# Attention and routed experts in one kernel: bias moved between scatter and return, a memset behind each return DMA, an unpaced scatter, and 13 attention batches ahead of the experts

## What is computed

```python
xn = layernorm(x)
q, k, v = split(xn @ w_qkv)                       # 16 heads of width 8
q_, k_ = exp(z - max(z)) with z = q @ proj, k @ proj   # 32 features per head
attn = (q_ @ (k_.T @ v)) / (q_ @ sum(k_) + 1e-6)
gates = sinkhorn((xn @ router_w.T + router_b) / temp, 3)
w, e = top_k(gates, 2)                            # weights normalised to sum 1
expert(t) = (relu(xn @ wg[e]) * (xn @ wp[e])) @ wo[e]
out = x + (attn @ w_out + b_out) + (xn + sum over the two experts of w * expert)
```

## Time and profile before

| | us |
|---|---|
| median of 3 runs | 329.74 (328.19 to 330.65) |
| the profiled execution | 327.3 |
| its span, first to last instruction | 325.5 |
| PE, DVE, ACT, POOL busy | 274.7, 222.9, 160.3, 237.6 |

### The profile page before, as it was taken

One profiled execution on the slowest core, in us unless ns is written; L12 is line 12 of the kernel. 1 busy time (PEld: TensorE's weight loads), 2 busy tenths in 40 slices (PEclk: granted clock), 3 DMA queues, 4 the chain that ended last, 5 costly groups with the idle time before them and its releaser, 6 DMA issues.

```text
span 325.5 us, 6627 instructions
## 1 busy us (share of the span) xinstructions
PE 274.7 (84%) x2044; PEld 257.5 (79%) x2044; DVE 222.9 (68%) x523; ACT 160.3 (49%) x365; POOL 237.6 (73%) x388
## 2 busy tenths in 40 slices
PE   5996878799999999999699999999999999850020
PEld 4896777689999999999599999999999999850010
DVE  4948889668888778888855777777777774500173
ACT  2774562134555555455346677777777775210000
POOL 5899520757888888888611688888888888888381
PEclk9998996589999999999979999999999999885555
DMA  7974000551111111111142598898888841111694
GB/s 236 339 272 164 4 0 0 167 191 45 47 50 52 45 49 46 47 50 51 36 110 61 166 244 245 244 256 251 245 246 248 251 134 48 42 49 40 226 383 174
DMA packets 32462, 45.22 MB, mean 139 GB/s; under 512 B 5328, under 2 KB 21200, under 8 KB 32432
## 3 DMA queue, kind: packets, MB, share of 16 engines
q1 hardware_dynamic: 26592, 33.83, 34.1%
q0 software_dynamic: 4544, 9.84, 9.0%
q10 hardware_dynamic: 1296, 1.20, 1.1%
HBM read 27.17 MB, written 17.68 MB: 138 GB/s over the span
## 4 chain that ended last, share of the span: by engine, by line
PE 49%; POOL 23%; DVE 12%; DMA 6%; issue 5%; ACT 2%; SPq 1%; ACTq 0%; POOLq 0%; DVEq 0%
POOL rows_y L541 17%; PE bank L642 7%; PE bank L666 6%; POOL acc L496 5%; PE bank L618 4%; PE bank L619 4%; PE bank L620 4%; PE bank L656 4%; PE bank L795 3%; DMA xn<-rows_y 2%; PE bank L591 2%; PE bank L783 2%; PE bank L574 2%; PE bank L784 2%; PE bank L785 2%
## 5 line engine op out<-in xcount | busy, mean ns | idle before, releaser
L541 POOL DMA_INDIRECT rows_y<-xn,row_i x78 | 80.5, 1032 | 28.2 <-ACT xn L969 15.1
L532 POOL DMA_INDIRECT slots_x<-xn,slot_i x64 | 63.9, 999 | 29.4 <-DVE slot_i L1195 10.1
L871 ACT ACTIVATE feat<-z_sb 128x512 f32<-128x512 f32 x64 | 39.9, 631 | 65.7 <-DVE z_sb L1065 65.7
L1058 DVE TENSOR_REDUCE neg_max<-bank 128x16 f32<-128x512 f32 x64 | 42.7, 684 | 19.8 <-PE bank L620 19.8
L783 PE MATMUL bank<-xT_high,w_high 128*128 128x256 f32 x156 | 47.3, 303 | 0.5 <-issue 0.5
L785 PE MATMUL bank<-xT_high,w_low 128*128 128x256 f32 x156 | 44.0, 282 | 0.0
L784 PE MATMUL bank<-xT_low,w_high 128*128 128x256 f32 x156 | 44.0, 282 | 0.0
L1065 DVE TENSOR_TENSOR z_sb<-bank,neg_max 128x512 f32<-128x512 f32 x64 | 42.6, 684 | 0.5
L795 PE MATMUL bank<-w_tile,hidden 128*128 128x128 f32 x312 | 41.0, 275 | 0.0
L642 PEld LDWEIGHTS bank<-v_aug,feat 128*128 128x128 f32 x256 | 31.5, 200 | 8.8 <-issue 7.4
L795 PEld LDWEIGHTS bank<-w_tile,hidden 128*128 128x128 f32 x312 | 38.2, 192 | 0.1
(11 more groups left out here) (145 smaller groups left out, 562.5 us busy)
## 6 DMA issues: line engine op xcount, KB each, us to landing
w_tile<-w_expert_dram SPq DMA_DIRECT2D x39, 384.0 KB
slots_x<-w_tile SPq DMA_DIRECT2D x39, 144.0 KB, 2.2
x_tile<-slots_x SPq DMA_DIRECT2D x39, 130.0 KB
acc<-x_dram SPq DMA_DIRECT2D x8, 256.0 KB, 5.3
xn<-rows_y SPq DMA_DIRECT2D x8, 256.0 KB, 5.8
w_tile<-rows_y SPq DMA_DIRECT2D x8, 256.0 KB, 6.5
rows_y<-xn,row_i POOLq DMA_INDIRECT x78, 3.7
slots_x<-xn,slot_i POOLq DMA_INDIRECT x64, 2.3
```

The costliest lines, as they stand in the source:

```text
L532: pool.indirect_dma_start(slots_x, bass.IndirectOffsetOnAxis(slot_i[k][:, i:i + 1], 0), xn[:, j, :], None).then_inc(scattered[n % FLIGHT], 16)
L541: pool.indirect_dma_start(rows_y, bass.IndirectOffsetOnAxis(row_i[:, k, t:t + 1], 0), y_tile(k, t), None)\
L871: act.activation(feat[par][n][:, :], z_sb[n][:, :], ACT.Exp).then_inc(feat_ready, 1)
L1058: dve.tensor_reduce(neg_max[n][:, :], args(n), AX_X, ALU.max, negate=True).then_inc(z_negmax, 1)
```

## The change

EARLY is 13 rather than 14. The scatter has no wait on `z_shifted` any more. `add_bias` adds the bias to a group of four tiles at once (eight calls of 128x512 in place of 64 of 128x64), all between the scatter and the first return, each call waiting for the attention additions that lie in its tiles and before (`acc_added`, at most 12). Behind each of the 78 return DMAs stands a memset and nothing else. `add_projection` waits for all eight bias groups at batch 12 only, and DVE's wait for the bias ahead of its combination is gone.

```diff
--- before.py
+++ after.py
@@ -58,13 +58,10 @@
     GROUP = 4
     NG = NT // GROUP
     BY_ACT = 2
-    LOOP_FROM = 2
     LINKS = 8
-    EARLY = 14
+    EARLY = 13
     FLIGHT = 4
     SETTLED = 24
-    PER_TWO = 10
-    LEAD = 1
     YR = 16
     UP = 3
     DX = D + 16
@@ -94,7 +91,7 @@
         scan_keep = sb("scan_keep", [P, E, NT])
         spare_row = sb("spare_row", [P, 2 * SLOT_TILES])
         eps_tile = sb("eps_tile", [P, 1])
-        gap = sb("gap", [P, SLOT_TILES])
+        gap = sb("gap", [P, 2 * SLOT_TILES])
 
         acc = sb("acc", [P, NT, D])
         xn = sb("xn", [P, NT, DX])
@@ -490,10 +487,10 @@
                 j, cols = half_tile(n)
                 pool.tensor_tensor(acc[:, j, cols], acc[:, j, cols], xn[:, j, cols], ALU.add).then_inc(base_added, 1)
 
-            def add_bias(n):
-
-                j, cols = half_tile((n + 4 * (EARLY - 1)) % (2 * NT))
-                pool.tensor_tensor(acc[:, j, cols], acc[:, j, cols], b_out_sb[:, cols], ALU.add).then_inc(bias_added, 1)
+            def add_bias(g):
+
+                tiles = acc[:, g * GROUP:(g + 1) * GROUP, :]
+                pool.tensor_tensor(tiles, tiles, over_tiles(b_out_sb, GROUP), ALU.add).then_inc(bias_added, 1)
 
 
             pool.wait_ge(weights_landed, 16 * N_WEIGHTS)
@@ -528,7 +525,6 @@
                         second_choice(SETTLED, NT, 1)
                     if n >= FLIGHT:
                         pool.wait_ge(scattered[n % FLIGHT], 16 * (n // FLIGHT))
-                    pool.wait_ge(z_shifted, 4 * LOOP_FROM - LEAD + 8 * n // PER_TWO)
                     pool.indirect_dma_start(slots_x, bass.IndirectOffsetOnAxis(slot_i[k][:, i:i + 1], 0),
                                             xn[:, j, :], None).then_inc(scattered[n % FLIGHT], 16)
                     add_xn(n)
@@ -540,17 +536,17 @@
                 for t in range(2):
                     pool.indirect_dma_start(rows_y, bass.IndirectOffsetOnAxis(row_i[:, k, t:t + 1], 0), y_tile(k, t), None)\
                         .then_inc(y_sent[k % YR], 16)
-                    n = 2 * k + t
-                    for piece in range(n * NT // SLOT_TILES, (n + 1) * NT // SLOT_TILES):
-                        add_bias(piece)
-                pool.memset(gap[:, k:k + 1], 0.0)
+                    pool.memset(gap[:, 2 * k + t:2 * k + t + 1], 0.0)
 
             pool.wait_ge(base_added, 2 * NT)
+            for g in range(NG):
+                pool.wait_ge(acc_added, min(GROUP // 2 * (g + 1), EARLY - 1))
+                add_bias(g)
             pool.wait_ge(acc_added, EARLY - 1)
             for k in range(SLOT_TILES):
                 send_rows(k)
 
-            pool.wait_ge(bias_added, 2 * NT)
+            pool.wait_ge(bias_added, NG)
             pool.wait_ge(acc_added, GROUP // 2 * (NG // 2))
             for n in range(NG // 2):
                 for k in range(TOPK):
@@ -1095,8 +1091,8 @@
             def add_projection(b):
                 dve.wait_ge(proj_ready, b + 1)
                 dve.wait_ge(base_added, 4 * b + 4)
-                if late(b, EARLY - 1):
-                    dve.wait_ge(bias_added, 2 * NT - 4 * (EARLY - 1))
+                if b == EARLY - 1:
+                    dve.wait_ge(bias_added, NG)
                 tiles = acc[:, bass.ds(2 * b, 2), :]
                 dve.tensor_tensor(tiles, bank[QT_BANK][:, 0:2 * P].rearrange("p (t d) -> p t d", t=2), tiles, ALU.add)\
                     .then_inc(acc_added, 1)
@@ -1314,7 +1310,6 @@
 
             for b in range(EARLY, NB):
                 step(b, b // 2, b % 2, front=b + 1 < NB)
-            dve.wait_ge(bias_added, 2 * NT)
             combine_group(0)
             denominators(NB - 1)
             invert(NB - 1)
```

## The result

The changed kernel took 339.3 us (median; 337.7 to 343.5) where the kernel before took 329.0 (327.9 to 330.7): 1.027 times its time, 95% interval 1.019 to 1.036. It is slower, though the interval leaves open whether by 2%. Foretold was 306. The rows of a run are from one recorded execution, and in `wide_memset`, `add_behind` and `add_1` further down that one was among the slower of its kernel (331.5, 327.6 and 350.9).

What follows compares the result with a forecast made beforehand. POOL's returns were taken to bound the kernel, and attention after the change: DVE free at 288.1 + 7.0 + 2.0 = 297.1, plus 5.1 to the span's end (302.2), 1.8 and 2.4, giving 306; range 302.5 to 310.

Steps and rivals of the forecast that it cites:

- New: every distance is 1.29, a pair 2.58, against PE's 2.545 a tile: Returns beside the experts: return DMAs 1.29 us apart, so POOL walks almost beside PE instead of falling behind 0.6 a tile.
- EARLY 13 and the scatter: Before the experts: they start 7.85 us earlier; without its wait the last scatter starts at 154.6, 9 us earlier.
- Bias in one place: Between scatter and first return: eight bias calls take 10.3 us, replacing 23.9, hidden in idle time with 2 to 3 left.
- The return: POOL's returns: third at 174.9, 75 distances of 1.29 are 96.8, plus 2.5 for holds; last starts at 274.1.
- The end: DVE's combination: attention, not the return, is late; DVE ends at 297.1, the span 5.1 later at 302.2.
- The own range: Whole kernel: the main forecast's median lies between 302.5 and 310 us, given 72%.
- Held every tile: Rival, returns beside the experts: DVE holds POOL's DMAs 0.6 in all 37 pairs, 22 us, median 323; at half, 312; 10%.
- The scatter's pace is its own: Rival, scatter: something other than the wait sets its pace, last scatter stays at 163.5, end some 8 later, median 314; 7%.
- Row loads late: Rival, experts' row loads: added latency makes PE wait; half a us more gives 314 (8%), 1.5 us more gives 331 (3%).
- 0.93 for faster: Whole kernel: the chance given that the change is faster by over 1%; within 1% had 0.03, slower 0.04.

Runs made afterwards that it cites:

- wide_memset: The changed kernel with a 128x256 memset behind each return DMA instead of the one-column memset, on chip A; its recorded execution took 331.5 us.
- add_behind: The changed kernel with a 128x64 addition, both inputs in SBUF, behind each return DMA instead of the memset, first on chip A; recorded execution 327.6 us.
- add_1: The changed kernel with a one-column addition behind each return DMA instead of the memset, on chip D; its recorded execution took 350.9 us.
- after_again: The changed kernel, unmodified, run again on chip C: 302.6 us.
- memset_320_2: The changed kernel with a 128x320 memset behind each return DMA, second run, on chip B (batch B2): 320.5 us.
- add_128: The changed kernel with a 128x128 addition behind each return DMA instead of the memset, on chip B (batch B2); time not given in the text.
- unpaced_before: The kernel before with only the scatter's wait on attention taken out, on chip C: 0.997 times the kernel before.
- no_memset: The changed kernel without the memsets behind the return DMAs, on chip A; time not given, 30 tiles held.
- copy_behind: The changed kernel with a one-column SBUF copy behind each return DMA instead of the memset, on chip B (batch B1); time not given in the text.
- half_rows: The changed kernel returning only half of each row, the other half left out of the output, on chip B (batch B1); time not given, 32 tiles held.
- add_behind_3: The changed kernel with the 128x64 addition behind each return DMA instead of the memset, run on chip B (batch B2): 322.7 us.

## Why the prediction was wrong

**The step that failed** is "New: every distance is 1.29, a pair 2.58, against PE's 2.545 a tile". The first half is right, the returns are 1.26 to 1.27 apart wherever they have work. The second carries PE's tile over from a trace in which no more than one distance in six was 1.29, each followed by longer ones, to a kernel in which all are. PE's tile was 3.37 us on average. Over the experts that is the 32.4 us above, 38 distances of 0.85 more than on C, and no term of the sum and no rival stood for it. What was wrong is thus the wait: the sum let PE run at its own pace, while PE's signals reached ACT up to 2.81 us late, so that PE in turn stood for the copies of ACT and DVE. So it was on three chips of four. On C the step holds (a tile of 2.52). The path by which the signals are held back stays open.

**Point by point, against the first profile and after_again on chip C.**

- *EARLY 13 and the scatter*: foretold last scatter 154.6, first transposition 162.7. Measured 155.48 and 164.3; on C 154.21 and 162.61. Right.
- *Bias in one place*: foretold 10.3 us, hidden. Measured 9.90 and 9.92, with 4.59 and 4.12 us of cover left. Right.
- *The return*: foretold third return at 174.9, last at 274.1. On C 174.49 and 270.57. The 2.5 us for DMAs stretched by DVE were not needed, as the mean of 961 ns shows (before 1032); no return of 78 was over 1.1 us long, before 11 were. In the first profile: 176.20 and 303.1. Wrong there.
- The Trainium skill (SBUF — State Buffer, "Who interferes with whom") would have put that loss at the low end, since the memsets only write. What it says of memsets is so here: of 78 in memset_320_2 none took over 0.394 us (median 0.380), while 13 of the 78 additions of add_128 were held, up to 0.999 (median 0.470). But the loss did not sit in what stood between the returns. It sat in the indirect DMAs themselves, 11 long ones of 78 behind those memsets as before the change, each of them beside DVE's `weights_low`; why none of after_again was long, with 46 beside `weights_low`, no run shows.
- *The end*: foretold that attention and not the return ends last, DVE at 297.1, span 302.2. On C DVE ended at 296.55 and the span is 298.8; the 5.1 from DVE's end to the span's end, taken over from before, were 2.3. Right in mechanism.
- *The own range* of the forecast, 302.5 to 310, is met on C by 0.1 us (302.6), and the ratio is the 0.93 that was foretold; part of that is luck, since the kernel before was there itself 4.3 us quicker than the 329.7 I reckoned against. In the other two batches with the unmodified kernel the median is missed by 33 and 34 us.

The end of the combination on C, timeline of DVE, where the earlier trace rows had 19.86 us of idling for a plane:

```profile
288.48 0.42 DVE L1097 TENSOR_TENSOR acc<-bank,acc 128x256 f32<-128x256 f32 x1 [4.34 <-PE bank L678]
288.82 0.75 DVE L324 TENSOR_TENSOR acc<-xn,acc 128x512 f32<-128x512 f32 x1
...
296.12 0.43 DVE L1097 TENSOR_TENSOR acc<-bank,acc 128x256 f32<-128x256 f32 x1
```

**The rivals.** *Held every tile* named the right place, POOL's pair as long as PE's tile, but the wrong victim: it let DVE stretch POOL's DMAs, while it was PE's signals that came late beside POOL's DMAs. *The scatter's pace is its own* is refuted by 154.59 in unpaced_before. *Row loads late*, the slower side, is not what happened: ACT waits in the rows above for PE's signal, and PE for copies of rows that it had long transposed, not for `x_tile`; and with half the returned bytes as many tiles were held. What 0.93 for faster left out: the trace of before nowhere sustains the new pace, so the price of sustaining it had no upper bound in it, and a rival that crosses zero should have stood there.

**What would be the better kernel.** add_behind beats the kernel before on three chips, by 0.980, 0.992 (under 1%) and 0.981, and keeps the other edits. It was not run on B1 or D, where attention suffered, so it is not known to be safe there. On C the change as it stands is far better (0.930).

## What to carry to other kernels

Work on GpSimd between two indirect DMAs may look like a cost on the queue that ends last and be the spacing that keeps the rest of the core in step: before taking it out, put a dummy of the same length in its place, and take away its length and its function one at a time. A rate that a trace shows singly is no evidence for that rate sustained. When a change to an off-path engine comes out wrong, look at the distance between a producer's end and its consumer's start, tile by tile, and repeat on another chip before building on either answer.

## What the runs showed of the hardware

- With indirect DMAs from GpSimd 1.26 to 1.46 us apart, ACT started 21 to 35 of 39 tiles over 0.3 us behind PE on three of four chips (41 to 58 us in sum, up to 4.1 for one), and none on the fourth (0 of 39 at 1.27). Where every signal is recorded (first profile, no_memset, copy_behind, half_rows) 18 to 22 of 39 came late, up to 2.97 us.
- The time of one and the same kernel was 339.3 us (chip not known), 339.8 (B) and 302.6 (C), while that of the kernel before differed by 1% (329.1 on B, 325.4 on C). Another was at 343.5 and 320.5 on one chip, B, at two times.
- An indirect DMA of 128 rows occupied GpSimd for 0.96 us, whether a row had 128 elements or 64 (half_rows, 1.26 apart as well), and for 0.98 to 0.99 where additions stood between. All long ones (over 1.1 us: 11 in the kernel before, 17 in add_behind_3) ran beside DVE's subtractions of 128x512 with both inputs in SBUF (`weights_low`); GpSimd's memsets were never stretched (0.394 us at most for 128x320, median 0.380).
- Eight additions of 128x512 that GpSimd makes undisturbed take 1.24 us each (9.90 for 8), where the nearest row before had 1.28.
